# Row maxima of an attention sent in half batches, and ten weight fills moved into the end of the batch before

## What is computed

```python
q = (Q @ w_q.T).reshape(B, S, G, HG, HD)
k = (K @ w_k.T).reshape(B, S, G, HD)
v = (V @ w_v.T).reshape(B, S, G, HD)
scores = jnp.einsum('bnghd,bmgd->bnghm', q, k) / scale
scores = jnp.where(causal, scores, NEG_INF)
attn = jax.nn.softmax(scores, axis=-1)
out = jnp.einsum('bnghm,bmgd->bnghd', attn, v).reshape(B, S, D)
return out @ w_o.T + b_o
```

## Time and profile before

| | us |
|---|---|
| median of three runs (lowest, highest) | 358.45 (357.24, 358.63) |
| the profiled execution, its time | 358.16 |
| its span, first to last instruction | 356.4 |
| the rest of its time | 1.76 |

### The profile page before, as it was taken

How to read it: one execution, slowest core, us unless ns; L and a number is a source line. 1 busy time by engine, 2 the same in 40 slices (tenths; PEclk the granted TensorE clock), 3 DMA queues, 4 the chain that set the end, 5 groups by cost and what they waited for, 6 DMA issues and landing times.

```text
span 356.4 us, 5063 instructions
## 1 busy us (share of the span) xinstructions
PE 317.8 (89%) x1639; PEld 217.8 (61%) x1639; DVE 257.8 (72%) x572; ACT 162.9 (46%) x333; POOL 108.7 (31%) x156
## 2 busy tenths in 40 slices
PE   2899885679999987999899999998979999999997
PEld 1494675556899644555544554553444886788885
DVE  3448886775777659999967996895672479999921
ACT  2432464434444312147767766775884344333000
POOL 6602675171000275501443325243554001000000
PEclk9999999559999999999999999999999999999999
DMA  7999200026111224600000000000000000000101
GB/s 205 361 413 312 63 1 16 13 92 202 65 61 61 75 73 138 262 0 9 0 7 2 1 0 9 0 3 3 5 3 0 2 0 0 2 0 0 47 29 44
DMA packets 14090, 22.96 MB, mean 64 GB/s; under 512 B 2065, under 2 KB 11409, under 8 KB 13202
## 3 DMA queue, kind: packets, MB, share of 16 engines
q1 hardware_dynamic: 13298, 20.56, 17.0%
q0 software_dynamic: 768, 2.10, 1.8%
HBM read 16.36 MB, written 6.03 MB: 63 GB/s over the span
## 4 chain that ended last, share of the span: by engine, by line
PE 57%; DVE 20%; issue 7%; POOL 6%; DMA 5%; ACT 4%; SPq 0%; DVEq 0%; ACTq 0%; POOLq 0%
PE bank L272 40%; DVE mx L1333 8%; PE bank L492 5%; PE bank L460 3%; ACT region L1009 3%; POOL x_sorted L806 2%; DVE stats L1079 2%; PE bank L463 2%; DMA region<-y_sorted,place 2%; PE bank L288 2%; POOL rstd L774 2%; DVE x_sb L1119 1%; PE bank L507 1%; DMA x_sb<-in_x_dram 1%; PE bank L282 1%
## 5 line engine op out<-in xcount | busy, mean ns | idle before, releaser
L1009 ACT ACTIVATE region<-bank,padcol 128x512 f32<-128x512 f32 x96 | 62.3, 693 | 18.6 <-PE bank L272 17.7
L1333 DVE TENSOR_REDUCE mx<-bank 128x2 f32<-128x512 f32 (+1 forms) x96 | 61.0, 683 | 4.7 <-PE bank L463 4.4
L842 POOL TENSOR_SCALAR_AFFINE_SELECT region<-region 128x1024 f32<-128x1024 f32 x32 | 35.9, 1122 | 77.8 <-ACT region L1009 77.7
L272 PE MATMUL bank<-qst,kblk 128*128 128x512 f32 x96 | 45.7, 487 | 0.7 <-DMA qst<-nmT 0.2
L460 PE MATMUL bank<-kblk,qst 128*128 128x512 f32 x96 | 43.5, 470 | 1.9 <-DVE mx L1333 1.5
L463 PE MATMUL bank<-causb,identb 128*128 128x256 bf16 (+1 forms) x96 | 30.6, 319 | 0.0
L272 PE MATMUL bank<-e_down,region 128*128 128x256 f32 x128 | 28.0, 380 | 0.0
L1119 DVE SCALAR_TENSOR_TENSOR x_sb<-bank,tg,x_sb 128x256 f32<-128x256 f32 x24 | 11.6, 483 | 21.0 <-PE bank L272 21.0
L272 PEld LDWEIGHTS bank<-e_down,region 128*128 128x128 f32 x128 | 24.2, 190 | 3.6 <-DVE region L1482 0.3
L770 POOL TENSOR_SCALAR veps<-mv 128x1 f32<-128x1 f32 x40 | 12.8, 321 | 42.5 <-DVE mv L1081 39.5
L774 POOL TENSOR_TENSOR rstd<-veps,power 128x1 f32<-128x1 f32 x40 | 24.8, 619 | 3.3
(11 more groups left out here) (195 smaller groups left out, 735.1 us busy)
## 6 DMA issues: line engine op xcount, KB each, us to landing
e_gu<-in_e_gu_dram SPq DMA_DIRECT2D x2, 1408.0 KB, 12.2
x_sorted<-zero SPq DMA_DIRECT2D x1, 1920.0 KB, 9.5
y_sorted<-region SPq DMA_DIRECT2D x15, 128.0 KB, 1.7
x_sb<-in_x_dram SPq DMA_DIRECT2D x4, 256.0 KB, 4.5
ctxT<-in_ctxT_dram SPq DMA_DIRECT2D x2, 512.0 KB, 6.7
e_down<-in_e_down_dram SPq DMA_DIRECT2D x1, 1024.0 KB, 14.1
region<-x_sorted SPq DMA_DIRECT2D x1, 1024.0 KB, 7.4
e_gu<-in_f_gate_dram SPq DMA_DIRECT2D x1, 1024.0 KB, 4.7
```

What stands on the lines that cost most here:

```text
L272: return pe.matmul(dst, lhsT, rhs, start=first, stop=last)
L842: pool.affine_select(out=block, in_=block, compare_op=ALU.is_ge, fill=0.0, base=0, pattern=[[0, 2], [0, PER_GROUP], [1, P]], channel_multi ...
L1009: taken(act.activation(dst, src.rearrange("p (h n) -> p h n", n=SEQ - mt * P), ACT.Exp, bias=padcol[:, key:key + 1], scale=float(HD) ** -0 ...
L1333: taken(dve.reduce_max(mx[:, b % 2, nt, quads, q, hg], src, AX), "sa")
```

## The change

The maxima travel by half batches. DVE negates half 0 after score fill 11 and half 1 after fill 23, with four operations each time on 16 columns in place of 32. PE transposes both tiles of a half into one bank, and ACT copies them with one instruction of 32x256. SP's queue issues two DMAs for each half, and waits before them until the DMAs of the half before have landed. `weights` waits for its half alone. In batch 0 the first turn stands after score fill 13, the second after the third leading fill of batch 1. In the loop the turn of half 0 of the next batch stands at n = 15, that of half 1 at n = 18 (batch 0) and n = 22 (others). `nmx` and `nmT` have one buffer for each half, in place of one for each parity of the batch.

Ten weight fills of batch 0 leave the loop: fills 0 to 2 stand beside score fills 21 to 23 of batch 0, and fills 3 to 9 beside the seven leading score fills of batch 1. Steps 0 to 9 of the loop of batch 0 then hold score fills alone; from step 10 on nothing of the weight fills is moved. In ACT's queue the copies of the four pieces of the stack of batch 1 alternate with the first exponentials.

```diff
-NEGATE_AT, FIRST_NEGATE_AT = 22, 18
+HALF_FILLS, EARLY_AT = 12, 21
+NEGATE_AT, FIRST_NEGATE_AT = (15, 22), (15, 18)
@@ PE
-            def neg_turn(b, kinds):
-                s = b % 2
+            def neg_turn(b, q):
+
+                half = 2 * b + q
+                dst = acquire(pe, "nmT", half, "turn1")
+                pe.wait_ge(sem("nm_made"), 2 * half + 2)
                 for nt in range(2):
-                    dst = acquire(pe, "nmT", 2 * b + nt, kinds[nt])
-                    pe.wait_ge(sem("nm_made"), 2 * b + nt + 1)
-                    ready(pe.transpose(dst[0:2 * HEADS, 0:P], nmx[:, s, nt, :].bitcast(F32), ident[:, :]), "nmT")
+                    ins = pe.transpose(dst[0:HEADS, tile_cols(nt)], nmx[:, q, nt, :].bitcast(F32), ident[:, :])
+                ready(ins, "nmT")
@@ weights
-                if n == 0:
-                    pe.wait_ge(sem("max_rows"), 16 * 2 * (b + 1))
+                if n % HALF_FILLS == 0:
+                    pe.wait_ge(sem("max_rows"), 16 * 2 * (2 * b + q + 1))
@@ PE, the order
                 scores(0, n)
                 if n in (1, 3):
                     stack_piece(0, 2 + n // 2, "exp")
+                if n == HALF_FILLS + 1:
+                    neg_turn(0, 0)
+                if n >= EARLY_AT:
+                    weights(0, n - EARLY_AT)
                 queries(1, n)
                 if n >= 20:
                     stack_piece(1, n - 20, "exp")
             for n in range(FIRST_LEAD):
                 scores(1, n)
+                weights(0, 24 - EARLY_AT + n)
                 if n == 2:
-                    neg_turn(0, ("turn1", "tok1"))
+                    neg_turn(0, 1)
             for b in range(BATCH):
                 lead = LEAD if b else FIRST_LEAD
+                done = 0 if b else 24 - EARLY_AT + FIRST_LEAD
                 for n in range(24):
                     if b + 1 < BATCH and n + lead < 24:
                         scores(b + 1, n + lead)
-                    weights(b, n)
+                    if n >= done:
+                        weights(b, n)
...
-                    if n == (NEGATE_AT if b else FIRST_NEGATE_AT) and b + 1 < BATCH:
-                        neg_turn(b + 1, ("turn1", "turn1"))
+                    if n in (NEGATE_AT if b else FIRST_NEGATE_AT) and b + 1 < BATCH:
+                        neg_turn(b + 1, int(n > NEGATE_AT[0]))
@@ SP
-            for b in range(BATCH):
-                sp.wait_ge(sem("nmT_taken"), 2 * b + 2)
+            for half in range(BATCH * HALVES):
+                b, q = divmod(half, HALVES)
+                sp.wait_ge(sem("nmT_taken"), half + 1)
+                if half >= 1:
+                    sp.wait_ge(sem("max_rows"), 16 * 2 * half)
@@ ACT
+            def neg_turn(b, q):
+
+                half = 2 * b + q
+                if b >= 1:
+                    act.wait_ge(sem("max_rows"), 16 * 2 * (half - 1))
+                src = filled(act, "nmT", half)[0:HEADS, 0:SEQ]
+                taken(act.activation(nmT[:, q, :], src, ACT.Copy), "nmT")
@@ ACT, the order
             for n in range(24):
+                if n == HALF_FILLS + 1:
+                    neg_turn(0, 0)
+                if n >= EARLY_AT:
+                    exponentials(0, n - EARLY_AT)
                 queries(1, n)
-            query_stack(1)
-            neg_turn(0)
+                if n >= 20:
+                    stack_copy(1, n - 20)
+            for n in range(FIRST_LEAD):
+                exponentials(0, 24 - EARLY_AT + n)
+                if n == 2:
+                    neg_turn(0, 1)
@@ DVE
                 taken(dve.reduce_max(mx[:, b % 2, nt, quads, q, hg], src, AX), "sa")
-
-            def negate(b):
+                if n % HALF_FILLS == HALF_FILLS - 1:
+                    negate(b, q)
```

More of the change, by code:

```diff
@@ L743, in _ @@
             load(sp, "f", f_down, a["f_down"])
-            for b in range(BATCH):
-                sp.wait_ge(sem("nmT_taken"), 2 * b + 2)
+            for half in range(BATCH * HALVES):
[3 more added lines that the diff above has]
+                    sp.wait_ge(sem("max_rows"), 16 * 2 * half)
                 for piece in range(2):
[L748 to L751, removed]
+                    rows = slice(piece * HEADS // 2, (piece + 1) * HEADS // 2)
+                    sp.dma_start(qst[24 + piece:P:32, b % 2, q, :, :].bitcast(F32), nmT[rows, q, :].bitcast(F32))\
                       .then_inc(sem("max_rows"), 16)
@@ L942, in queries, with stack_copy @@
                 act.activation(qhi[:, s, :, :], src, ACT.Copy).then_inc(sem("q_high"), 1)
-            def query_stack(b):
[L945 to L953, removed]
+            def stack_copy(b, piece):
+                q, h = divmod(piece, 2)
+                stage, i = stack_fill(b, piece)
+                src = filled(act, stage, i).rearrange("p (h n) -> p h n", h=2)
+                if b >= 2:
+                    act.wait_ge(sem("sb_ready"), 24 * (b - 1))
+                taken(act.activation(qst[:, b % 2, q, 2 * h:2 * h + 2, :], src, ACT.Identity, bias=small_c[:, 0:1]), "qs")
+            def query_stack(b):
+                for piece in range(0 if b < 2 else 2, 4):
+                    stack_copy(b, piece)
             loaded(act, "e_down", 3)
@@ L1032, in _ @@
             for n in range(24):
+                if n == HALF_FILLS + 1:
+                    neg_turn(0, 0)
+                if n >= EARLY_AT:
+                    exponentials(0, n - EARLY_AT)
                 queries(1, n)
-            query_stack(1)
-            neg_turn(0)
+                if n >= 20:
[4 more added lines that the diff above has]
+                    neg_turn(0, 1)
             for b in range(BATCH):
+                done = 0 if b else 24 - EARLY_AT + FIRST_LEAD
                 for n in range(24):
-                    exponentials(b, n)
+                    if n >= done:
+                        exponentials(b, n)
                     if b >= 1 and n % 2 == 1:
@@ L1044, in _ @@
                         ln_turn(3, NORM_STEPS.index(n))
-                    if n == (NEGATE_AT if b else FIRST_NEGATE_AT) and b + 1 < BATCH:
-                        neg_turn(b + 1)
+                    if n in (NEGATE_AT if b else FIRST_NEGATE_AT) and b + 1 < BATCH:
+                        neg_turn(b + 1, int(n > NEGATE_AT[0]))
                 if b + 2 < BATCH:
@@ L1333, in row_maxima, with negate @@
                 taken(dve.reduce_max(mx[:, b % 2, nt, quads, q, hg], src, AX), "sa")
-            def negate(b):
[L1337 to L1340, removed]
-                for nt in range(2):
[L1342 to L1346, removed]
+                if n % HALF_FILLS == HALF_FILLS - 1:
+                    negate(b, q)
+            def negate(b, q):
+                half = 2 * b + q
+                dve.wait_ge(sem("sa_taken"), 24 * b + HALF_FILLS * (q + 1))
+                if b >= 1:
+                    dve.wait_ge(sem("nmT_ready"), half - 1)
+                for nt in range(2):
+                    m = mx[:, b % 2, nt, :, q, :]
+                    high, low = (nmx[:, q, nt, c:c + HEADS // 2].rearrange("p (j h) -> p j h", j=QUADS) for c in (0, HEADS // 2))
+                    dve.tensor_scalar(high, m, -1.0, None, ALU.mult).then_inc(sem("nm_high"), 1)
+                    dve.wait_ge(sem("nm_high"), 2 * half + nt + 1)
+                    dve.scalar_tensor_tensor(out=low, in0=m, scalar=-1.0, in1=high.bitcast(F32), op0=ALU.mult,
                                              op1=ALU.subtract).then_inc(sem("nm_made"), 1)
@@ L1417, in _ @@
                 queries(1, n)
-            negate(0)
             for b in range(BATCH):
```

12 lines of the change are left out of this document (2 added, 10 removed).

## The result

The changed kernel takes 364.91 us (median of four runs, 363.49 to 365.20) against 358.54 us for the kernel before beside it: a ratio of 1.0175, with a 95% interval of 1.0147 to 1.0203. The direction was forecast; the size was not. 361.9 us was predicted, with 364.0 as the upper end.

What follows compares the result with a forecast made beforehand. The prediction took DVE's row maxima to bound the head, with PE setting the pace in two places. Its terms, 0.73 + 2.2 - 0.35 - 0.2 + 1.3 = +3.7 on 358.16, gave 361.9 us, range 357.3 to 364.0.

Steps and rivals of the forecast that it cites:

- What bounds the head: Head of the attention, 141 to about 178 us: DVE's maxima set the pace, 0.60 us each, PE in two places.
- Rival (c): Faster: the whole head stays at DVE's pace and the new order hides; 355.5 us, chance 0.13.
- Term 1: First turn of batch 0, after score fill 13: PE waits for half 0's negation, so DVE resumes late; +0.7 us.
- Term 2: ACT's queue between stack pieces and first exponentials: table load and alternating order delay batch 1's first score fill; +2.2 us.
- Rival (a): Table loaded in ACT's idle time before piece 0, out of the chain; 360.9 us, chance 0.12.
- rival (d): A drain of some 1.38 us beside the table load; 363.3 us, chance 0.03.
- Term 3: Loop of batch 0, steps 0 to 16: added negation against less waiting for PE and a shorter normalisation; -0.35 us.
- Term 4: Turns of half 1: two transposes into one bank skip a wait for ACT; -0.6 in batches 1 and 2, -0.2 in batch 0.
- Term 5: Turn at step 15 of batches 1 and 2: PE waits until DVE has taken the finish in the same bank; +1.0 each.
- The added negations of batches 1 and 2: Negations of half 0 of batches 2 and 3, where PE and DVE are level: +0.2 each, between 0 and 0.64.
- Rival (b): PE's lead covers the new waits at step 15 of batches 1 and 2; 359.8 us, chance 0.22 with smaller kin.
- (e): PE's clock falls to its lower level because PE waits several times between 156 and 161 us; 364.5 us, chance 0.03.

Runs made afterwards that it cites:

- mends_no_early: Changed kernel, ten early fills back in the loop, half 0's turn at step 14, batches 2 and 3's negation behind maximum 14, first turn behind score fill 16: 358.03 us.
- mends_table_at_5: Changed kernel with the three moves of mends_no_early, early fills kept, and the exponential's table loaded at step 5 of the head: 358.88 us, ratio 1.0007.
- table_early: Changed kernel with a one-column exponential behind ACT's copy of batch 1's query projection, so the table loads in idle time: 362.27 us, ratio 1.0128.
- one_bank_turn: Kernel before with only both transposes of a turn in one bank and one ACT copy of 64x256, maxima still by whole batches: 357.19 us, ratio 0.9974.
- turn_at_14: Changed kernel with the turn of half 0 at step 14 of the loop in place of 15: 362.78 us, ratio 1.0134.

## Why the prediction was wrong, point by point

- **What bounds the head: right.** DVE's maxima at 0.60 us with PE in between for the projection and the pieces. mends_no_early against mends_table_at_5 shows that ten weight fills taken off PE are worth nothing there. Rival (c) fell.
- **Term 1: right**, +0.91 from the first maximum for +0.73, inside its bound of 0.95. From the landmark it reads +0.63, which flatters it by the 0.28 us of the untouched piece.
- **Term 2: right in size and cause.** +2.19 us on PE in the four steps for 2.05, split by table_early in 1.43 for the load and 0.76 for the fills. The first score fill of batch 1 came 4.0 later than in the earlier trace rows, of which 1.15 is the late start, so 2.8, as walked. Without the load I gave the term 1.2, and ascribed what is left to ACT's alternating order. But no wait for ACT stands in the four steps of table_early, so the 0.76 left in them is PE's own work. Rival (a) is out. So is rival (d): the load starts 0.02 us behind the copy ahead of it and ends at 159.52, and the exponential starts at 159.53, with no drain on either side. The Trainium skill (page "ScalarE: Activation LUTs", section "What ACT_TABLE_LOAD costs") counts a drain of about 1.38 us with every switch; this trace does not show it.
- **Term 3: right in sum**, as far as the rows separate it from terms 2 and 4, but one sentence of it carries the failure: that none of the added negations lies behind a full group of exponentials. I walked batch 0 only. In batches 1 and 2 the added negation stands in DVE's queue at step 7, and the eighth exponential completes a group there, so the select starts 0.3 us ahead of it.
- **Term 4: right.** -0.41 and -0.62 for -0.6 each, and one_bank_turn shows it alone.
- **Term 5: the turn at step 15 right**, +0.97 and +1.12 for 1.05 each. turn_at_14 gives back only half, for the reason above. **The added negations of batches 1 and 2: the step that failed.** I took +0.2 each, with 0.64 as the upper end, on the ground that DVE has idle time some steps later. They cost +1.09 and +1.32. Two things were wrong in it. The four operations take not 0.64 but 1.21 us, as the first waits for the select. And the idle time of DVE some steps later does not help, because PE waits at `finish(b-1, 4)` behind that very negation (1.16 us) and brings the delay along. That is 2.0 of the 2.4 us by which the sum was short (2.7 from the first maximum). Even a negation of 0.64 would have cost about 0.7 there by the estimate above, so the cover failed as well as the length. The rule on the select was quoted in the prediction, and its case was read from the wrong batch.
- **Rival (b) fell**, since the waits of 0.71 and 1.13 us stand before the turns of step 15. (e) fell too: in the changed kernel the granted clock reads 1.00 in every stretch from 130 to 280 us, and what PE lost are the waits named.
- **The range** left out this cost, since its bound came from rows of a negation that met no select, although three of the four in the trace before did (first operations of 0.80, 0.48 and 0.78 us). The first of the three is the very next negation after the one whose rows I used (DVE, kernel before, maxima of batch 1):

```profile
177.44 0.80 DVE L1343 TENSOR_SCALAR nmx<-mx 128x32 fp32r<-128x32 f32 x1
```

With 1.2 in place of 0.64 for each of the two, the upper end of 364.0 would have been 365.1 and held the time. But 364.0 itself is not a sum of the bounds: term 2 at its upper bound gives 363.2, and so do terms 4 and 5 at the 2.6 that was stated for them, where their own parts add up to 2.2. So 0.8 us of the range has no source.

## What to carry to other kernels

Work that is moved out of a stretch is worth what its engine is waited for there, and costs what its engine is waited for where it goes: find that stretch by stretch, in start-to-start distances, before adding up. A small operation between large ones costs its wait as well as its length; look for what the other engines run at that step in every batch, since the cover differs from one to the next. And a transposing turn that puts both of its transposes into one bank for one copy saves a round trip between two engines, 0.6 us a turn at step 22, at no cost that these traces show.

## What the runs showed of the hardware

- A tensor_scalar of DVE on 16 columns took 0.17 us alone and 0.79 us when it started during a select of POOL of 1.09 us; it ended 0.04 us after the select. Half the columns hardly make it shorter: 0.17 to 0.18 us for 32. The Trainium skill (page "SBUF — State Buffer", section "Who interferes with whom") says that DVE in a two-port mode, which a tensor_scalar can enter, and GpSimd lock each other out for a whole instruction; the trace agrees. The other operation of the negation waits too: in batch 2 one took 1.00 us in place of 0.17 (changed kernel, at 250.16, against a select from 250.05 to 251.14).
- The execution as a whole moves more than its parts. In the thirteen profiles of kernels whose code ahead of the attention is the same, the landmark started between 128.52 and 131.35 us, while the stretch that follows repeated within 0.2 us for the kernel that was profiled twice. Its own untouched first piece ranged over 0.45 us, so a landmark should stand as close as possible to the first thing that was changed. Single microseconds of a change are read from such stretches of the trace, not from a median.
